# A graph layer on one core: zeros stored behind the load of the destinations, parameters prepared in two parts

## What is computed

```
h    = relu(layernorm(x))                       # no parameters
xn   = layernorm(h) * g1 + b1
msg  = relu(xn[src] + edge_attr)                # 25000 edges, dst sorted
aggr = segment_sum(msg, dst, 50000)
t    = (1 + eps_gin) * xn + aggr
t    = relu(t @ Wg1 + bg1) @ Wg2 + bg2
h2   = h + t
f    = gelu(layernorm(h2; g2, b2) @ Wf1 + bf1) @ Wf2 + bf2     # 128 -> 512 -> 128
out  = x + h2 + f
```

## Time and profile before

| what | value |
|---|---|
| median of 3 runs (lowest, highest) | 1072.53 us (1070.97, 1072.89) |
| the profiled execution | 1073.02 us, its span 1071.3 us |
| PE busy | 992.9 us, 93% |
| DVE busy | 978.7 us, 91% |
| ACT busy | 844.3 us, 79% |
| POOL busy | 799.9 us, 75% |
| bytes moved by DMA | 156.87 MB, mean 146 GB/s |

### The profile page before, as it was taken

The page is one execution under the profiler, slowest core; times in us unless marked ns, Lnnn a source line. Parts: engine busy times, 40 slices in busy tenths (PEclk is TensorE's granted clock), DMA queues, the critical chain, the costliest instruction groups (busy, mean ns, idle before and its releaser), DMA issues. The chain is left out here.

```text
span 1071.3 us, 23085 instructions
## 1 busy us (share of the span) xinstructions
PE 992.9 (93%) x6684; PEld 850.1 (79%) x6684; DVE 978.7 (91%) x3499; ACT 844.3 (79%) x2158; POOL 799.9 (75%) x510
## 2 busy tenths in 40 slices
PE   1336999999999999999999999999999999999998
PEld 1225888888888888888888888888888888878887
DVE  5577999999999999999999999999999999988752
ACT  1247888888888888888888888888888888878773
POOL 6488787787787787887887877888878878866610
PEclk9858999999999999999999999999999999999999
DMA  7566676788887655555555554555565654443311
GB/s 234 139 189 161 161 191 185 177 245 233 234 242 216 134 135 130 135 135 127 138 136 123 138 142 118 139 142 117 142 140 114 143 141 112 120 102 92 58 57 40
DMA packets 110469, 156.87 MB, mean 146 GB/s; under 512 B 24836, under 2 KB 50608, under 8 KB 110335
## 3 DMA queue, kind: packets, MB, share of 16 engines
q1 hardware_dynamic: 70358, 128.99, 37.6%
q0 software_dynamic: 37760, 25.66, 19.3%
q10 hardware_dynamic: 2216, 0.66, 0.3%
HBM read 90.61 MB, written 64.61 MB: 145 GB/s over the span
## 5 line engine op out<-in xcount | busy, mean ns | idle before, releaser
L520 ACT ACTIVATE n_act<-p_f,bf1e_col 128x512 f32<-128x512 f32 x392 | 255.9, 679 | 149.4 <-PE p_f L875 141.5
L447 POOL DMA_INDIRECT aggr_sums<-e_merged,e_index x196 | 322.8, 1647 | 65.8 <-issue 49.8
L917 PE MATMUL p_out<-wf,n_act 128*128 128x128 f32 x3136 | 370.6, 276 | 0.0
L917 PEld LDWEIGHTS p_out<-wf,n_act 128*128 128x128 f32 x3136 | 357.6, 191 | 4.0
L456 POOL TENSOR_TENSOR n_rstd<-n_var,minus_half 128x12 f32<-128x12 f32 (+2 forms) x102 | 256.4, 2514 | 116.4 <-DVE n_var L827 59.6
L436 POOL DMA_INDIRECT e_x<-in_x,e_cols x196 | 214.6, 1095 | 61.6 <-issue 58.9
L875 PE MATMUL p_f<-n_z2T_high,wf_low 128*128 128x512 f32 x392 | 207.0, 528 | 11.9 <-issue 7.0
L875 PE MATMUL p_f<-n_z2T_high,wf_high 128*128 128x512 f32 x392 | 154.6, 395 | 0.0
L875 PE MATMUL p_f<-n_z2T_low,wf_high 128*128 128x512 f32 x392 | 153.9, 393 | 0.0
L672 DVE BATCH_NORM_STATS2 n_stat<-n_x 128x6 f32<-128x256 f32 x392 | 139.6, 415 | 0.1
L532 ACT ACTIVATE p_gout<-n_relu,n_rstd 128x128 f32<-128x128 f32 x392 | 129.3, 367 | 5.4 <-DVE n_x L799 5.2
(11 more groups left out here) (85 smaller groups left out, 1433.5 us busy)
## 6 DMA issues: line engine op xcount, KB each, us to landing
n_x<-in_x SPq DMA_DIRECT2D x97, 256.0 KB
n_aggr<-aggr_sums SPq DMA_DIRECT2D x97, 256.0 KB
out_dram<-n_out SPq DMA_DIRECT2D x97, 256.0 KB
aggr_sums<-zeros SPq DMA_DIRECT2D x26, 512.0 KB, 3.2
e_dst<-in_dst_rows SPq DMA_DIRECT2D x49, 256.0 KB
e_attr<-in_attr SPq DMA_DIRECT2D x48, 256.0 KB
aggr_sums<-zeros SPq DMA_DIRECT2D x12, 1024.0 KB
e_x<-in_x,e_cols POOLq DMA_INDIRECT x196
```

What stands on the lines that cost most here:

```text
L447: nc.gpsimd.indirect_dma_start(out=aggr, out_offset=bass.IndirectOffsetOnAxis(ap=e_index[0:r, s, j:j + 1], axis=0), in_=e_merged[0:r, s, j ...
L520: nc.scalar.activation(n_act[:, k, :, 0:b.rows], p_f[k % 2][:, :, 0:b.rows], ACT.Gelu, bias=bf1e_col[:, k:k + 1]).then_inc(s_act, 1)
L917: last = nc.tensor.matmul(p_out[0:b.rows, j, :], n_act[:, k, j, 0:b.rows], wf2[:, k, :], start=False, stop=(k == KF - 1), skip_group_check ...
```

## The change

Two things are moved. On SP, the first four zero stores go right behind the load of `o_dst`, without the wait for chunk 1's gather: ahead of the attributes of chunk 1, the ends of chunk 2 and the attributes of chunk 2. On DVE, `prepare_parameters` is cut in two. Its first four instructions now run ahead of `half_chunk`; the rest, `finish_parameters`, runs at the end of DVE's step in which block 1 is the newest (step 1). The waits for its results go to the first instruction that uses each: `s_bias` to the first `p_g` on PE and the first `n_gT` on ACT, `s_wf1` = 4 and `s_bf1` to the first `p_f` on PE, `s_bf1` to the first gelu on ACT.

```diff
@@ SP, prologue
             sp.dma_start(o_dst[:], dst_rows).then_inc(s_order_in, 16)
+            sp.wait_ge(s_zeros, 1)
+            set_to_zero(range(zero_halves_begun(-1)))
             first_chunks(step, *range(1, LEAD - 1))
-            sp.wait_ge(s_zeros, 1)
-            sp.wait_ge(q_gather[1], 16 * J)
-            set_to_zero(range(zero_halves_begun(-1)))
             first_chunks(step, LEAD - 1)
@@ ACT, gelu and hidden
                     reached(act, s_fout, b.at)
+                    if b.is_number(0):
+                        act.wait_ge(s_bf1, 1)
...
                 reached(act, s_gout, b.at - 1)
+                if b.is_number(0):
+                    act.wait_ge(s_bias, 1)
@@ ACT, prologue
             half_chunk(step)
-            act.wait_ge(s_bias, 1)
-            act.wait_ge(s_bf1, 1)
             branch(act, EDGE_LAG, 6, step)
@@ DVE, prepare_parameters
                                         ALU.mult).then_inc(s_scaled_params, 1)
+            def finish_parameters():
                 dve.wait_ge(s_wf1, 1)
@@ DVE, end of step, and prologue
                     second_half(edge(1), edge(2), node, apart)
+                if (b := first) is not None and b.is_number(1):
+                    finish_parameters()
             first_chunks(step, *range(LEAD))
+            prepare_parameters()
             half_chunk(step)
-            prepare_parameters()
             dve.wait_ge(s_scaled_params, 2)
@@ PE, first_product, step (at p_g) and prologue
                     reached(pe, s_act, b.at * KF + k - 1)
+                    if b.is_number(0) and k == 0:
+                        pe.wait_ge(s_wf1, 4)
+                        pe.wait_ge(s_bf1, 1)
...
                     reached(pe, s_gT, b.at)
+                    if b.is_number(0):
+                        pe.wait_ge(s_bias, 1)
...
-            pe.wait_ge(s_bias, 1)
-            pe.wait_ge(s_wf1, 4)
             pe.wait_ge(s_const, 8)
```

## The result

| kernel | median | lowest to highest | runs |
|---|---|---|---|
| before | 1072.89 us | 1070.97 to 1073.06 | 5 |
| after | 1067.46 us | 1065.76 to 1069.48 | 5 |

The ratio is 0.9954 with an interval of 0.9939 to 0.9969: faster by 4.9 us by the ratio, 5.4 by the medians, where 9.5 were forecast. The profiled execution took 1065.76 us (span 1064.0), the fastest of the five; a second profile further down took 1067.52.

The account below looks back on a forecast made before the run. The ramp up to PE's first p_f, headed by the parameter wait, was taken to set the time. e_merged 9.5 us earlier gave 1073.02 - 9.5 = 1063.5, the median 0.49 lower: 1063.0 us, range 1060.5 to 1069.5.

Parts of the forecast that it names:

- What bounds the kernel: Fixed pace from 200 us; the ramp to PE's first p_f (98.16 us) sets the end, headed by the parameter wait.
- The waits at the branch: On ACT, without the parameter wait, e_merged of chunk 0 starts at 31.3 instead of 39.42 us, gaining 8.1 us.
- The zeros: Earlier SP stores: chunk 0 lands 1.4 us later, chunk 1 2.15 us later, chunk 2 at 27.5 instead of 28.92.
- the 5.80 us of landing: Time from a chunk's last gather issue to its use beside zeros, taken from chunk 2, applied to chunks 0 and 1.
- The two parts of the preparation: On DVE, 0.98 us and 2.08 us, both hidden in idle time before gathers; cost 0, else their own length.
- The sum: e_merged at 29.9 us, 9.5 us earlier, carried through POOL, gathers, DVE and first p_f to the end: 1063.0 us.
- A (the stores go first): Gather packets get no turn between zeros; chunk 0 lands 5.0 us later, gain 5.9 us, 1066.6; chance 0.20.
- B: PE at half clock for a whole step from first p_f costs 9.4 us, 1072.4; chance 0.10 with other near-total losses.

Follow-up runs that it names:

- a second profile further down: The changed kernel run and traced again with no edit; median 1067.17 us, ratio to before 0.9943.
- r8: Changed kernel with the second part of the preparation in step 0, ahead of the wait for chunk 3's gather; 1067.33 us, ratio to before 0.9944.
- r10: Changed kernel with 1.5 MB on SP issued behind chunk 2's gather, the finish in step 0 and two extra PE products; 1065.52 us, ratio to before 0.9924.
- r3: Kernel before with only the first zero stores moved earlier on SP, preparation as before; 1072.53 us, ratio to before 0.9993.

## Why the prediction was wrong, by its own steps

- **What bounds the kernel:** right. The start of the steady state sets the time, and a shift at 135 us is there at 916 us (5.98 and 6.02 us).
- **The waits at the branch:** right in place and size. e_merged came 8.4 us sooner with the parameters alone (8.1 forecast) and 9.17 with both parts (9.5).
- **The zeros:** right within their bounds. Chunk 0 was used 1.2 us later (1.4), chunk 2 at 27.99 (27.5). Chunk 1 needed no more delay than chunk 0 gave it: used at 18.76, where 19.7 was forecast, so the 5.80 us of landing did not hold for it.
- **The two parts of the preparation:** hidden, as r8 shows. The rule of the Trainium skill's page "SBUF — State Buffer" (the trap that DVE blocks DMA), that VectorE's copy would hold up GpSimd's descriptors, does not show as a cost here: POOL's scatter at 52.41, the one beside the finish (52.24 to 54.32), took 1.66 us, and the scatters of before up to 70 us took 1.55 to 1.76. In r8 and r10, where the finish falls beside the gather at 36.43 and 36.18, that gather took 1.24 us for 1.10, so 0.14 us at most.
- **The sum:** here it failed, at the path from e_merged to the first p_f. It carried the 9.5 us from e_merged through "POOL's queue, the gathers, DVE and PE's first p_f" because POOL's timeline named no other engine between 40.89 and 62.68. That was true of before. But the DMA engines were part of that chain, and their state at POOL's start was a gift of the long wait: in before, about 1 MB of SP's transfers had moved while POOL stood idle. Moved 9.2 us forward, the scatters met all 2 MB, and POOL paid 4.69 us instead of 0.85. Of the 9.5 us forecast at the first p_f 6.5 were left. A sign of it stood in the timeline of before: the gap ahead of the third scatter was 0.85 us, not the usual 0.31, and in r3, where it is 0.99, it ends with the landing of the first scatter pair. So there was no slack in that landing even before the change. The prediction asked what is late next after the wait and named chunk 2's landing; it did not ask what else had used the idle time.
- **The rivals:** the time, 1067.46, lies where A (the stores go first) had put it, and so within the stated range, but that is luck: A did not happen, since chunk 0 would have been used at 18. The collision is of A's kind, between SP's queue and POOL's, one stage later and with scatters instead of gathers. B was half right: the first p_f did run at half clock, but the lead only fell from 6.5 to 6.0 us between it and 135 us, where 9.4 was the fear; the runs do not isolate the clock's share.

Some of the loss came back: before, POOL waited 1.82 us for its scatter at 67.24, after, 0.78 of plain issue at 61.35, so the lead grew from 4.9 to 5.9 us. In the second trace it was 6.3 and then 6.2. What stays open is the spread. Among the after runs the time varied by 3.7 us, and the profiled one gained 1.3 us more near 950 us, at the last chunks, where the second trace gained 0.5; these are not explained.

## What to carry to other kernels

A wait that stalls one engine is idle time for the DMA queues as well, and other transfers use it. Before counting a removed wait in full, list what the other queues issue in the time into which the work moves. Here the preparation's gain was real, 9.2 us at POOL's first scatter, and over a third of it was lost until 1.5 MB of SP's transfers were issued ahead of that scatter, behind the last gather.

## What was not expected of the hardware

- A pair of scatters of 128 rows each, issued by 35.65 us, held up the next until 43.10 beside 2 MB of SP's transfers, and cost no such wait (under 0.4 us) with 1.5 MB of them sent earlier. In four microseconds POOL's queue got 126 packets of 0.5 KB through beside 492 of 1.9 KB, and 332 in about the same stretch of before, gathers among them.
- ACT's issue of the large parameter loads slowed when SP's zeros were queued; both rows are Wg1 and Wg2 on ACT's own queue, before and after:

```profile
5.03 1.02 ACTq L615 DMA_DIRECT2D wg<-in_Wg  x2
```

```profile
5.71 2.69 ACTq L618 DMA_DIRECT2D wg<-in_Wg  x2
```

With the zeros moved alone (r3) the pair took 3.03 us, with the parameters alone (r2) 1.02. It cost nothing here, as ACT's first work on a chunk began at 15.33 us, behind chunk 0's landing.
